# Macaron block on one core: q and k rows by frequency and then head, one store for each unit, half of the first heads loaded later

## The chip, the cores and the metric

One core of one Trainium2 chip runs the whole program. The metric is the device time of one execution in microseconds (us).

## The reference

Input x is [2, 2048, 256]. LN is a layer norm without weights.

```
x = x + 0.5 * ffn(LN(x))          # 16 experts, each takes its 256 best tokens, and a shared expert
x = x + attn(LN(x))
x = x + 0.5 * ffn(LN(x))

attn: q, k, v = x @ W.T + b, 16 heads of 16; q, k rotated by position (cos, sin of 8 frequencies, halves of a head paired)
      att = softmax(causal(q k^T / 4));  y = att v;  return y @ Wo.T + bo
```

## The kernel before

The change lies in attention, which has three blocks of code: `projections`, `exact_shift` and `attention`. Each block ends with a barrier of all engines.

`projections` walks over 8 quads of 512 tokens (`q`). VectorE takes the statistics of a quad two ahead (`statistics`, L1350), ScalarE normalizes it (`normalize`), TensorE transposes it, ScalarE copies the columns (`columns`) and VectorE subtracts the copy for the low part (`low_columns`, L1371), since every product is made of three matmuls with high and low parts (`product3`, L182 to L184). TensorE then makes four tiles of rows, `rows(4q)` to `rows(4q + 3)`: the first halves of q's heads, the second halves, and the same for k. VectorE rotates them (`rotate`, L1383) into `turns`. A unit `n = 2q + a` (a = 0 for q, 1 for k) is two such tiles: GpSimd forms the two sums (`turned`, L1448 and L1449), ScalarE makes the high half (`high`, L1308), GpSimd the low half (`low`, L1453), for the last three units VectorE instead (L1415), and SP stores the unit (`store`, L1190) into `q_rows` or `k_rows` in memory, in four transfers of 256 KB. Four units are in flight in `half`. The rows in memory lie head by head: 32 rows for a head, 16 high and 16 low, each 2048 tokens (8 KB) long.

SP works through one queue. For each q it first issues `load(q + 3)`, the x of the quad three ahead, which waits for the normalizing of quad q; then `store(2q)` and `store(2q + 1)`, which each wait for the low half. After each store of q = 4 and 5 it loads one of the four heads of attention's group 0 (`load_head`, L1590, and `load_shift`, L1602): 32 and 16 rows into 48 partitions, for q and for k. The rows of batch 0 are all stored by then.

At the end VectorE takes the largest squared norm of all heads (`largest`, L1423 to L1429) and leaves a flag `unsafe`. `exact_shift` is a guarded stage: SP, GpSimd, VectorE and TensorE read the flag and jump over the stage if it is 0, which it is for these inputs. Its loop over all 32 heads would compute exact maxima.

`attention` has 8 groups of 4 heads and for each 4 blocks of 512 queries. A unit is a set of scores (L1826, L1834) that ScalarE turns into exponentials (L1905); the scores of a unit wait for the exponentials of the unit three before. Block 0 of group 0 has 5 units, block 1 has 13, so block 2 begins at unit 18. Block 0 and 1 read columns 0 to 1023 of queries and keys only. SP waits for GpSimd to clear the buffer of group 1 and loads group 1, then the output weights, the biases and four residuals; group g is loaded when group g - 2 has had its scores.

## Time and profile before

| | |
|---|---|
| median of 3 runs | 1627.05 us |
| lowest and highest | 1625.15 and 1629.43 us |
| the profiled execution, its time | 1620.89 us |
| its span in the trace | 1619.2 us |
| mean granted clock of TensorE | 0.983 |
| busy: TensorE, ScalarE, VectorE, GpSimd | 93%, 61%, 55%, 35% |

Busy time is the time covered by instructions of an engine. [...] Engines in rows: PE is TensorE's matmul, PEld its weight load, DVE VectorE, ACT ScalarE, POOL GpSimd, SPq the queue on which SP issues transfers.

### The profile page before, as it was taken

What the parts mean: (1) busy time and instruction counts of PE and PEld (TensorE: products, weight loads), DVE (VectorE), ACT (ScalarE), POOL (GpSimd) and SP (SyncE); (2) the same over time, 40 slices, a digit from 0 to 9 for tenths busy, and PEclk for the clock granted to TensorE, in tenths of its full rate; (3) what the DMA queues carried; (4) which work ended last, traced back from release to release, by engine and by line L of the source; (5) the groups of instructions that cost most, each with busy time, mean ns of one, the idle gap of its engine ahead of it and who ended that gap; (6) DMA issues with size and microseconds to landing.
All of it is one profiled execution on the core that took longest, in us unless ns stands there. A gap on an engine that the chain in (4) does not pass through costs nothing. (4 is left out here: it accounts for less than half of the span.)

```text
span 1619.2 us, 26554 instructions
## 1 busy us (share of the span) xinstructions
PE 1508.0 (93%) x9945; PEld 1048.4 (65%) x9945; DVE 888.3 (55%) x1946; ACT 981.1 (61%) x1330; POOL 559.4 (35%) x498
## 2 busy tenths in 40 slices
PE   4899999999995878999999999999799999999997
PEld 3788889889884663333333333333588888898886
DVE  6787666667655771133043421212788757676663
ACT  7322254454434768999999999999532225544542
POOL 3000245665635872111011111110300035656644
PEclk9999999999997997999999999999999999999999
DMA  8231166666634799225054352210422136666753
GB/s 282 65 99 53 51 166 148 156 146 154 152 65 130 219 239 229 41 42 81 7 103 85 121 84 38 43 53 27 145 71 96 49 103 154 149 151 151 154 130 39
DMA packets 121552, 181.04 MB, mean 112 GB/s; under 512 B 19600, under 2 KB 83600, under 8 KB 118288
## 3 DMA queue, kind: packets, MB, share of 16 engines
q1 hardware_dynamic: 92960, 130.57, 31.0%
q0 software_dynamic: 28464, 48.78, 14.8%
q8 instruction: 79, 1.29, 0.4%
q14 instruction: 49, 0.40, 0.1%
HBM read 123.73 MB, written 55.57 MB: 111 GB/s over the span
## 5 line engine op out<-in xcount | busy, mean ns | idle before, releaser
L1905 ACT ACTIVATE 8072_pr<-8072_pS 128x1024 f32<-128x1024 f32 x448 | 421.2, 1073 | 12.9 <-PE 8072_pS L1826 11.6
L1856 PE MATMUL 8072_pO<-8072_pr,6212_vres 128*32 128x512 f32 x1792 | 240.3, 606 | 4.9 <-DVE 8072_tO L1930 3.8
L1826 PEld LDWEIGHTS 8072_pS<-sq_rows,sk_rows 50*128 50x128 f32 x896 | 74.5, 185 | 198.0 <-ACT 8072_pr L1905 153.4
L1826 PE MATMUL 8072_pS<-sq_rows,sk_rows 50*128 50x512 f32 x896 | 185.1, 465 | 8.3 <-ACT 8072_prs L1905 4.1
L1930 DVE STREAM_TRANSPOSE 8072_tO<-8072_pO 128x512 f32<-128x512 f32 (+1 forms) x33 | 23.0, 698 | 265.2 <-PE 8072_pO L1856 265.2
L182 PE MATMUL 112_pGU<-columns_XT,weights_wts 128*128 128x512 f32 x384 | 153.0, 398 | 1.6 <-DVE columns_XT L917 1.6
L182 PE MATMUL 15018_pGU<-columns_XT,weights_wts 128*128 128x512 f32 x384 | 152.5, 397 | 1.6 <-DVE columns_XT L917 1.6
L1919 POOL TENSOR_SCALAR_AFFINE_SELECT 8072_pr<-8072_pr 128x512 f32<-128x512 f32 x32 | 21.4, 670 | 376.0 <-ACT 8072_pr L1905 375.9
L183 PE MATMUL 112_pGU<-columns_XT,weights_wts 128*128 128x512 f32 x384 | 150.1, 391 | 0.0
L184 PE MATMUL 112_pGU<-columns_XT,weights_wts 128*128 128x512 f32 x384 | 150.0, 391 | 0.0
L183 PE MATMUL 15018_pGU<-columns_XT,weights_wts 128*128 128x512 f32 x384 | 149.8, 390 | 0.0
L184 PE MATMUL 15018_pGU<-columns_XT,weights_wts 128*128 128x512 f32 x384 | 149.8, 390 | 0.0
L764 ACT ACTIVATE hidden_hT<-15018_hf 128x512 fp32r<-128x512 f32 x96 | 60.7, 632 | 145.0 <-DVE 15018_hf L907 145.0
L764 ACT ACTIVATE hidden_hT<-112_hf 128x512 fp32r<-128x512 f32 x96 | 60.7, 632 | 144.7 <-DVE 112_hf L907 144.7
L1079 POOL DMA_INDIRECT out<-15018_eo,15018_idx x64 | 109.4, 1709 | 98.6 <-issue 67.1
L1079 POOL DMA_INDIRECT x_after_ffn<-112_eo,112_idx x64 | 109.4, 1709 | 98.2 <-issue 66.7
L182 PE MATMUL 112_pD<-weights_wts,hidden_hT 128*128 128x256 f32 x376 | 108.7, 289 | 1.4 <-DVE hidden_hT L912 1.4
L182 PE MATMUL 15018_pD<-weights_wts,hidden_hT 128*128 128x256 f32 x376 | 108.7, 289 | 1.4 <-DVE hidden_hT L912 1.4
L907 DVE TENSOR_TENSOR 15018_hf<-15018_gl,15018_pGU 128x512 f32<-128x512 f32 x96 | 65.9, 686 | 75.6 <-PE 15018_pGU L184 46.4
L907 DVE TENSOR_TENSOR 112_hf<-112_gl,112_pGU 128x512 f32<-128x512 f32 x96 | 65.9, 686 | 75.2 <-PE 112_pGU L184 45.7
L184 PE MATMUL 112_pD<-weights_wts,hidden_hT 128*128 128x256 f32 x376 | 106.3, 283 | 0.0
L184 PE MATMUL 15018_pD<-weights_wts,hidden_hT 128*128 128x256 f32 x376 | 106.3, 283 | 0.0
(370 smaller groups left out, 3419.9 us busy)
## 6 DMA issues: line engine op xcount, KB each, us to landing
112_raw_g<-WgT SPq DMA_DIRECT2D x16, 512.0 KB, 4.1
112_raw_u<-WuT SPq DMA_DIRECT2D x16, 512.0 KB, 3.6
112_raw_d<-WdT SPq DMA_DIRECT2D x16, 512.0 KB, 3.9
q_rows<-rows_half SPq DMA_DIRECT2D x32, 256.0 KB, 3.5
k_rows<-rows_half SPq DMA_DIRECT2D x32, 256.0 KB, 5.1
sq_rows<-q_rows SPq DMA_DIRECT2D x32, 256.0 KB
sk_rows<-k_rows SPq DMA_DIRECT2D x32, 256.0 KB
15018_raw_g<-WgT SPq DMA_DIRECT2D x16, 512.0 KB, 3.9
```

What stands on the lines that cost most here:

```text
L182: pe.matmul(out, w_hi, x_hi, start=start, stop=False)
L183: pe.matmul(out, w_hi, x_lo, start=False, stop=False)
L184: return pe.matmul(out, w_lo, x_hi, start=False, stop=stop)
L764: s_hh.done(a.activation(hT[0][:, i % 2, f, :], hf[:, f % 2, :], ACT.Copy))
L907: s_mul.done(v.tensor_tensor(hf[:, f % 2, :], gl[:, f % 2, :], pU(f % 2), ALU.mult))
L1079: s_sc[k].part(g.indirect_dma_start(out, bass.IndirectOffsetOnAxis(rows_[:, q:q + 1], 0), eo[:, k, q, :], None, compute_op=ALU.add), 16)
L1826: m = t_.matmul(to[:, e, :], key, query, start=True, stop=True)
L1856: m = t_.matmul(pO[e * 32:(e + 1) * 32, off:off + wd], vres[:, (g // GB) * TPB + kt, at:at + 32], from_(e), start=n == first[j], stop=n == ...
L1905: s_exp.done(a.activation(to, pS[:, u % RING, :, :], ACT.Exp, scale=HD ** -0.5))
L1919: s_mask.done(g.affine_select(out=blk_, in_=blk_, compare_op=ALU.is_ge, fill=0.0, base=0, pattern=[[0, GH], [1, P]], channel_multiplier=-1))
L1930: s_copy.done(v.transpose(tO[:, part], pO[:, part]))
```

## The change

- Rows come by frequency and then head. On the host, weights, biases and rope table are permuted (`by_half`, `c_rope`), and the mask that sums squares by head (`head_of`) is formed with a stride. In memory row r of head h now lies at r * 16 + h, so the rows of one head are 128 KB apart.
- A unit is stored in one transfer of 1 MB instead of four of 256 KB; `half` is one tensor, `both`.
- Quad 0 of x is loaded in two transfers instead of four; the rope table's last three parts share a semaphore, on which the second quad waits for all three.
- Of group 0's heads the projections load columns 0 to 1023 only. Attention issues the other columns as 16 transfers ahead of group 1, and the scores of group 0's block 2 wait for all of them (`s_rest`).
- The two sums of the last unit move from GpSimd to VectorE. VectorE's last work is in a new order: the sums, `low(13)`, the maxima, `low(14)`, the flag, `low(15)`.
- ScalarE ends the projections with a one-element exp.
- `exact_shift` writes its loop twice, once for each batch.

```diff
-        tab, ds = self.qk[a], self.bass.ds
+    def head_rows(self, a, b):
+        return self.qk[a].rearrange("(b n h) s -> b n h s", b=B, h=H)[b]
...
+        tab, ds = self.head_rows(a, b), self.bass.ds
         for lo, n in ((0, 2 * HD), (2 * HD, HD)) if a == 0 else ((0, HD), (HD, 2 * HD)):
-            eng.dma_start(dst[lo:lo + n, :].bitcast(self.f32), tab[ds(head * (2 * HD), n), :]).then_inc(sem, 16)
+            eng.dma_start(dst[lo:lo + n, :].bitcast(self.f32), tab[0:n, ds(head - b * H, 1), :]).then_inc(sem, 16)
...
-            half = [self.rows_at(f"half{h}", [P, KS, 2, W], f32r, 16 * 1024 * h) for h in range(2)]
+            both = self.rows_at("halves", [P, KS, 2, 2, W], f32r)
+            half = [both[:, :, h, :, :] for h in range(2)]
...
-                    for part in range(2):
-                        for u in range(2):
-                            dst = self.qk[a_].rearrange("(b h r u f) s -> b r u h f s", b=B, r=2, u=2, f=HD // 2)[bb][part][u]
-                            self.s_rows[n % KS].part(sp.dma_start(dst[:, :, cc * W:(cc + 1) * W],
-                                                                  half[part][:, n % KS, u, :].bitcast(f32)), 16)
-
-                for j in range(4):
-                    s_x0[j].done(sp.dma_start(xq[:, 0, j, :], xv[0][:, j, :]))
+                    dst = self.qk[a_].rearrange("(b n p) s -> b p n s", n=4, b=B)[bb]
+                    from_ = both[:, n % KS, :, :, :].rearrange("p h u w -> p (h u) w").bitcast(f32)
+                    self.s_rows[n % KS].done(sp.dma_start(dst[:, :, cc * W:(cc + 1) * W], from_))
+
+                for j in range(2):
+                    s_x0[j].done(sp.dma_start(xq[:, 0, 2 * j:2 * j + 2, :], xv[0][:, 2 * j:2 * j + 2, :]))
...
-                    s_trig[k].done(sp.dma_start(trig[:, :, part], self.ins["c_rope"][:, :, part]))
+                    s_trig[min(k, 1)].done(sp.dma_start(trig[:, :, part], self.ins["c_rope"][:, :, part]))
...
-                        if q in (4, 5):
+                        if (q, half_) in HEAD_AFTER:
+                            hh = HEAD_AFTER.index((q, half_))
                             sp.wait_ge(*s_clear.at(3))
                             sp.wait_ge(*s_zero.at(1))
-                            self.load_head(sp, 0, 2 * (q - 4) + half_)
-                            self.load_shift(sp, 0, 2 * (q - 4) + half_)
+                            self.load_head(sp, 0, hh, slice(0, S // 2), self.s_ld[0][hh // 2])
+                            self.load_shift(sp, 0, hh)
...
-                    a.wait_ge(*s_y.at(n + 1))
+                    a.wait_ge(*(s_y.at(n + 1) if n < 2 * J - 1 else s_last_y.at(1)))
...
                 high(2 * J - 1)
+                a.activation(warm[:, :], self.eps[0:1, :], ACT.Exp)
...
-                for n in range(POOL_LOW, 2 * J):
-                    self.s_rows[n % KS].wait(v, n // KS)
-                    low(n)
+                k = (2 * J - 1) % 3
+                s_turn.wait(v, 4 * J)
+                v.tensor_tensor(turns[k][:, 0, :], turns[k][:, 0, :], turns[k][:, 2, :], ALU.subtract)
+                s_last_y.done(v.tensor_tensor(turns[k][:, 1, :], turns[k][:, 1, :], turns[k][:, 3, :], ALU.add))
+                low(POOL_LOW)
                 largest(J - 1)
                 s_norm.wait(v, J // 2)
                 s_top.done(v.tensor_reduce(top[:, :], norm[:, :], AX.X, ALU.max))
+                low(POOL_LOW + 1)
...
                 s_flag.done(v.tensor_scalar(self.unsafe[:, :], prod[:, :], SAFE_NORMS, None, ALU.is_gt))
+                low(POOL_LOW + 2)
                 v.wait_ge(*s_flag.at(3))
...
-                for n in range(2 * J):
+                for n in range(2 * J - 1):
                     turned(n)
...
-                with eng.Fori(0, B * H) as h:
-                    body(h)
+                for b in range(B):
+                    with eng.Fori(b * H, (b + 1) * H) as h:
+                        body(b, h)
...
+                for hh in range(GH):
+                    self.load_head(sp, 0, hh, slice(S // 2, S), self.s_rest)
                 sp.wait_ge(*self.s_clear.at(4))
...
+                    if (g, blocks[j][1]) == (0, QB // 2) and "rest" not in arrived:
+                        arrived.add("rest")
+                        t_.wait_ge(*self.s_rest.at(1))
...
-    by_half = lambda w: w.reshape(H, 2, HF, -1).transpose(1, 0, 2, 3).reshape(D, -1)
+    by_half = lambda w: w.reshape(H, 2, HF, -1).transpose(1, 2, 0, 3).reshape(D, -1)
...
-        "c_rope": np.ascontiguousarray(np.tile(rope.transpose(2, 0, 1), (H, 1, 1))),
+        "c_rope": np.ascontiguousarray(np.repeat(rope.transpose(2, 0, 1), H, 0)),
```

## Rows read from the trace of the kernel before

**Rows 1.** The page's busy times: busy us (share of the span), instructions.

```profile
PE 1508.0 (93%) x9945; PEld 1048.4 (65%) x9945; DVE 888.3 (55%) x1946; ACT 981.1 (61%) x1330; POOL 559.4 (35%) x498
```

**Rows 2.** Timeline of VectorE in the loop: start, duration, instruction, [idle before, releaser].

```profile
537.93 1.41 DVE L1350 BATCH_NORM_STATS2 6217_st<-6217_xq 128x6 f32<-128x256 f32 x4 [1.34 <-DMA 6217_xq<-x_after_ffn]
...
540.74 1.29 DVE L1371 TENSOR_TENSOR sk_xT<-6217_pX,sk_xT 128x512 fp32r<-128x512 f32 x2 [0.85 <-ACT sk_xT L1297]
...
552.20 1.29 DVE L1371 TENSOR_TENSOR sk_xT<-6217_pX,sk_xT 128x512 fp32r<-128x512 f32 x2 [0.85 <-ACT sk_xT L1297]
...
562.16 1.41 DVE L1350 BATCH_NORM_STATS2 6217_st<-6217_xq 128x6 f32<-128x256 f32 x4 [1.21 <-DMA 6217_xq<-x_after_ffn]
...
564.97 1.29 DVE L1371 TENSOR_TENSOR sk_xT<-6217_pX,sk_xT 128x512 fp32r<-128x512 f32 x2 [0.85 <-ACT sk_xT L1297]
```

**Rows 3.** The loads of x, L1178: who waited for them, us, times.

```profile
  DVE 6217_st L1350: 2.8, 3
```

**Rows 4.** Timeline of VectorE, ScalarE, GpSimd and SP at the end of the projections.

```profile
600.82 1.21 DVE L1415 TENSOR_TENSOR rows_half<-sq_turns,rows_half 128x1024 fp32r<-128x1024 f32 x1
...
602.12 1.20 ACT L1316 ACTIVATE 6212_vres<-6217_pV 128x256 f32<-128x256 f32 x4
...
603.12 2.24 POOL L1449 TENSOR_TENSOR sq_turns<-sq_turns 128x512 f32<-128x512 f32 x1
...
606.55 1.22 DVE L1415 TENSOR_TENSOR rows_half<-sq_turns,rows_half 128x1024 fp32r<-128x1024 f32 x1 [2.31 <-ACT rows_half L1308]
607.69 0.68 DVE L1389 TENSOR_REDUCE 6217_norm<-6217_pN 128x1 f32<-128x512 f32 x1
607.80 2.48 SPq L1190 DMA_DIRECT2D k_rows<-rows_half  x4
...
609.53 0.14 DVE L1429 TENSOR_SCALAR 6212_unsafe<-6217_prod 1x1 int32<-1x1 f32 x1
```

**Rows 5.** Timeline at the start of attention, and where group 0 ends.

```profile
612.80 1.28 ACT L1905 ACT_TABLE_LOAD   x1 [6.35 <-PEq L1473]
...
612.84 1.22 PE L1826 MATMUL 8072_pS<-sq_rows,sk_rows 50*128 50x512 f32 x4 [3.84 <-PEq L1473]
...
614.10 1.94 ACT L1905 ACTIVATE 8072_pr<-8072_pS 128x1024 f32<-128x1024 f32 x2
...
631.70 0.73 PE L1826 MATMUL 8072_pS<-sq_rows,sk_rows 50*128 50x512 f32 x4
...
678.09 0.80 SPq L1590 DMA_DIRECT2D sq_rows<-q_rows  x2
```

**Rows 6.** Timeline of SP's queue: start and duration of the issues, how many.

```profile
500.05 0.59 SPq L1178 DMA_DIRECT2D 6217_xq<-x_after_ffn  x1
500.67 2.90 SPq L1200 DMA_DIRECT2D 6217_trig<-c_rope  x3
...
530.55 2.48 SPq L1190 DMA_DIRECT2D k_rows<-rows_half  x4
533.08 0.59 SPq L1178 DMA_DIRECT2D 6217_xq<-x_after_ffn  x1
```

**Rows 7.** Stretches: us, busy of each engine, granted clock, DMA share, GB/s.

```profile
531.75:532.00 0.25, 0.00 (x0) 0.00 (x0) 0.25 (x1) 0.25 (x1) 0.00 (x0) 1.00 0.98 221
534.25:534.50 0.25, 0.25 (x2) 0.19 (x1) 0.00 (x0) 0.25 (x2) 0.25 (x1) 1.00 0.55 180
...
600.90:612.80 11.90, 1.93 (x14) 0.93 (x12) 5.89 (x8) 3.48 (x7) 4.38 (x3) 0.73 1.04 332
612.80:627.05 14.25, 12.95 (x80) 5.64 (x80) 1.40 (x3) 12.68 (x13) 7.39 (x8) 0.63 0.95 205
618.00:638.00 20.00, 19.42 (x156) 6.79 (x156) 2.79 (x6) 17.94 (x20) 4.90 (x8) 0.86 1.02 151
```

**Rows 8.** Timeline at the barrier behind attention, where no guarded stage follows.

```profile
1141.94 1.55 SPq L1762 DMA_DIRECT2D x_after_attn<-rows_acc  x2
1143.90 1.28 ACT L719 ACT_TABLE_LOAD   x1 [10.32 <-PEq L1620]
```

More of the change, by code:

```diff
@@ L171, in scope, with load_stack @@
         return st
-    def load_stack(self, eng, dst, a, head, sem):
-        tab, ds = self.qk[a], self.bass.ds
+    def head_rows(self, a, b):
+        return self.qk[a].rearrange("(b n h) s -> b n h s", b=B, h=H)[b]
+    def load_stack(self, eng, dst, a, b, head, sem):
+        tab, ds = self.head_rows(a, b), self.bass.ds
         for lo, n in ((0, 2 * HD), (2 * HD, HD)) if a == 0 else ((0, HD), (HD, 2 * HD)):
-            eng.dma_start(dst[lo:lo + n, :].bitcast(self.f32), tab[ds(head * (2 * HD), n), :]).then_inc(sem, 16)
+            eng.dma_start(dst[lo:lo + n, :].bitcast(self.f32), tab[0:n, ds(head - b * H, 1), :]).then_inc(sem, 16)
     def product3(self, pe, out, w_hi, w_lo, x_hi, x_lo, start, stop):
@@ L1161, in projections @@
             s_n0 = sig("proj_act_first")
-            s_x0 = [sig(f"proj_x_first{j}", 16) for j in range(4)]
-            s_trig = [sig(f"proj_trig{k}", 16) for k in range(S // W)]
+            s_x0 = [sig(f"proj_x_first{j}", 16) for j in range(2)]
+            s_trig = [sig("proj_trig_first", 16), sig("proj_trig", 16)]
             s_T, s_Q, s_V, s_N, s_tt = (sig("proj_pe_" + n_) for n_ in ("T", "Q", "V", "N", "top"))
@@ L1168, in projections @@
             s_wh, s_wl, s_y, s_lo = (sig("proj_pool_" + n_) for n_ in ("wh", "wl", "y", "lo"))
-            s_last = sig("proj_dve_lo")
+            s_last, s_last_y = sig("proj_dve_lo"), sig("proj_dve_y")
             POOL_LOW = 2 * J - 3
+            HEAD_AFTER = ((4, 0), (4, 1), (5, 0), (5, 1))
             s_clear = self.s_clear
@@ L1378, in rotate @@
                     if n < 4 * (S // W):
-                        v.wait_ge(*s_trig[q].at(1))
+                        v.wait_ge(*(s_trig[1].at(S // W - 1) if q else s_trig[0].at(1)))
                     s_lo.wait(v, n // 2 - 2)
@@ L1393, in _ @@
                 with nc.allow_low_precision(reason="zeros and ones"):
-                    s_set.done(v.tensor_reduce(head_of[:, 0:H], self.ident[:, :].rearrange("p (h w) -> p h w", w=HD // 2), AX.X, ALU.add))
+                    s_set.done(v.tensor_reduce(head_of[:, 0:H], self.ident[:, :].rearrange("p (w h) -> p h w", h=H), AX.X, ALU.add))
                 statistics(0)
@@ L1505, in run, with head @@
                         self.s_ld[0][pair].wait(sp, 1)
-                    def head(h):
+                    def head(b, h):
                         sp.wait_ge(s_go, h + 1)
-                        self.load_stack(sp, qa, 0, h, s_ld)
-                        self.load_stack(sp, ka, 1, h, s_ld)
+                        self.load_stack(sp, qa, 0, b, h, s_ld)
+                        self.load_stack(sp, ka, 1, b, h, s_ld)
                         dve_h.wait(sp, "lo", h)
@@ L1535, in run, with head @@
                     v.sem_inc(s_go, 1)
-                    def head(h):
+                    def head(b, h):
                         v.wait_ge(s_ld, 64 * h + 64)
@@ L1563, in run, with head @@
                     t_.wait_ge(s_ident, 1)
-                    def head(h):
+                    def head(b, h):
                         with t_.Fori(0, TPB) as q:
@@ L1577, in _, with load_head @@
                 guarded(t_, run)
-    def load_head(self, sp, g, hh):
+    def load_head(self, sp, g, hh, cols, loaded):
         k, pair, base = g % 2, hh // 2, 64 * (hh % 2)
@@ L1586, in load_head @@
                 self.s_rows[n].wait(sp, self.stored(2 * NQ // B if g < 4 else 2 * NQ, n))
-        head, loaded = g * 4 + hh, self.s_ld[k][pair]
+        head = g * 4 + hh
         for a_, dst in enumerate((self.sq, self.sk)):
             for lo, n in ((0, 2 * HD), (2 * HD, HD)) if a_ == 0 else ((0, HD), (HD, 2 * HD)):
-                loaded.part(sp.dma_start(dst[base + lo:base + lo + n, k, pair, :].bitcast(self.f32),
-                                         self.qk[a_][head * 2 * HD:head * 2 * HD + n, :]), 16)
+                loaded.part(sp.dma_start(dst[base + lo:base + lo + n, k, pair, cols].bitcast(self.f32),
+                                         self.head_rows(a_, head // H)[0:n, head % H, cols]), 16)
     def stored(self, units, n):
@@ L2054, in attn @@
             self.unsafe = st.sb("unsafe", [1, 1], self.i32)
-            self.s_rows = [sig(f"rows_stored{k}", 64) for k in range(ROWS_RING)]
+            self.s_rows = [sig(f"rows_stored{k}", 16) for k in range(ROWS_RING)]
+            self.s_rest = sig("rest", 16 * 16)
             self.s_ld = [[sig(f"loaded{k}{pair}", 16 * 10) for pair in range(2)] for k in range(2)]
```

8 lines of the change are left out of this document (4 added, 4 removed).

## The prediction

> **What bounds the kernel now.** I read the page first [rows 1]: TensorE has records for 93% of the span, ScalarE for 61%. The edit touches the projections (496.56 to 610.28 us) and the first microseconds of attention, so the rest of the span can only be shifted. Then I read the stretches, the timeline of each engine and the waits in that part.
>
> Three things stand there. In the projections the quads follow each other through the two `low_columns` subtractions of VectorE: they start at 540.74 and 552.20, a period of 11.46 us, and at 564.97, a period of 12.77 us [rows 2]. The long period holds a wait of 1.21 us for the next 512 rows of x, an earlier one, at 537.93, a wait of 1.34 us [rows 2]; three such waits sum to 2.8 us [rows 3]. In the loop no other wait is for a transfer. At the end of the stage there is a chain: the GpSimd sum of the last unit (603.12, 2.24 us beside busy VectorE), ScalarE's high half right behind it at 605.4, VectorE's low half at 606.55, then four store issues of SP from 607.80 to 610.28. VectorE itself has its flag at 609.67. All engines start attention at 612.80, 2.52 us behind SP [rows 4, 5]. There the first exp stands behind a table load, although its scores were begun at 612.84 [rows 5].
>
> **The change, step by step.**
>
> *The store in one transfer.* SP issued four transfers a unit, 2.48 us together, and behind those of an odd unit the load of x [rows 6]. The new transfer has 512 pieces of 2 KB. Nearest rows: a load of 512 pieces of 1 KB took 0.59 us to issue, three of 256 pieces of 2 KB took 2.90 us, 0.97 each [rows 6]. I take 0.8 us; the bounds are 0.59 us and 2.48 us, if the issue goes by pieces as 4 x 0.62 does. So SP is free 1.7 us sooner for each unit.
>
> *The load of x that stands behind it.* It is issued 1.7 us sooner, but it need not land 1.7 us sooner, since its data come behind the data of the store. In the period read, the store was issued at 530.55, its data moved from 531.75 to about 534.2, the load was issued at 533.08, the share of the DMA engines dipped to 0.55 at 534.25 between the two, and VectorE went on at 537.93 [rows 2, 6, 7]. The megabyte of the store takes 2.5 us or more whoever issues it. So what is gained is the dip and the slow start behind it: 0.4 us at least. If the load then runs at the store's 2.5 us a megabyte, its data have moved at 535.5 and the whole wait (1.34, 1.21) goes. I take 0.9 us for each of the two waits and 0.2 for the third: **-2.0 us**, with bounds 0 (the issue isn't shorter, or the one big store holds the load back) and -3.1. The upper bound is the sum of waits, 2.8, and what the long periods are longer by beyond their wait, 0.1 each. That these microseconds reach the end: the period without a wait is 11.46 as it stands, and it needs nothing that the longer one doesn't.
>
> *First loads of x in two, the three later parts of the rope table on one semaphore.* Two issues take the place of four. The statistics read half a megabyte in the same order, and each half now lands in one. The gain of the last half and the loss of the first are each about one issue, 0.59 us at most [rows 6]. I take 0. The later rope parts are issued by 503.6, and the second quad turns more than ten microseconds later: 0. The head mask's reduction reads with a stride now; VectorE has idle time there till the first x lands: 0.
>
> *Row order.* Weights, biases, rope table and mask are permuted on the host, so no instruction of compute changes. What changes is that a head's 48 rows lie 128 KB apart instead of 8 KB. The loads of heads run at 151 GB/s with the share of the DMA engines at 1.02 [rows 7]; stores reach far more. I take the rate as unchanged. [...]
>
> *Last sums on VectorE.* Two 512-column sums cost half of the 1.21 us of a 1024-column subtraction [rows 4], 0.65 each with a start. From 600.82: sums to 602.2, low half of unit 13 to 603.4, maximum (0.68) and a short reduction to 604.3, low half of unit 14 to 605.5 (TensorE turns the tops under it), best, product and flag, three short ones of which the last took 0.14, to 606.2, low half of unit 15 to 607.4 [rows 4]. That last one needs ScalarE's high half, which stands behind the values' eviction (602.12, 1.20 us) and so ends at 604.4: covered. GpSimd drops out, so neither its 2.24 us nor a stretched subtraction occurs. SP issues at 607.4 and is done at 608.2 with 0.8 us; before it was 610.28. **-2.1 us**; bounds -2.3 (issue of 0.59) and -0.4 (2.48). Neither part does it alone: with the sums alone SP would end at 607.4 + 2.48 = 609.9, with the one transfer alone VectorE would be last, at 609.67.
>
> *Exp ahead of the barrier.* ScalarE is idle from 604.4 on, the load of 1.28 us and a one-element exp fit under the rest. At attention's start the first exp began at 614.10, 0.02 us behind the table load. Its scores are half of four matmuls that took 1.22 us from 612.84, so 613.5 [rows 5]. **-0.5 us**; bounds 0 (TensorE, at a low clock, then sets the pace) and -0.6. [...]
>
> *Second halves of the columns moved behind the barrier.* 16 transfers (4 heads x 2 x 2) with 1.57 MB leave the projections and go ahead of group 1 in attention. In the projections nothing waited for them, so nothing is gained there but a shorter backlog of stores (share 1.04 from 600.90 to 612.80 [rows 7]). In attention the queues passed are: SP's own for group 1 (20 issues, held back by GpSimd's clear), then the output weights and four residuals. Two issues of this kind take 0.80 us [rows 5], so the 16 take 6.4; the data of group 1, 3.15 MB and 21 us at 151 GB/s, come behind. It is first needed when group 0 has had its scores, at 678.09 [rows 5]; by this rate all has landed by 644. Covered by over 30 us. The second halves are needed by unit 18, at 631.70 less 2.6, so 629.1 (the loop's gain shifts both sides alike). The second halves are issued from 610.7, move behind the last store from about 611.9, and 1.57 MB at 151 GB/s are 10.4 us: landed at 622.6. Covered by 6 us: 0.
>
> *Guarded stage with its loops written twice.* It is skipped, but its code is jumped over. The barrier with it takes 2.52 us; the one behind attention, without a guarded stage, 0.41 (from 1141.94 + 1.55 to 1143.90) [rows 8]. The 2.1 us between is what the test and the jump cost. A few dozen more instructions lie under it: 0, bounds -0.3 and +0.5.
>
> *Clock.* [...] ScalarE is idle for 1.57 of the 14.25 us of the stretch in attention [rows 7], which is all that the low clock can cost it there; I take 0, bounds -0.8 and +0.8.
>
> **Sum.** -2.0 - 2.1 - 0.5 = -4.6 us. The profiled execution took 1620.89 us with a span of 1619.2, so it would be 1616.3. It lies 6.16 us under the median of the runs shown, 1627.05; the median would be 1622.4, faster by 0.28%. About 0.3%, 4.9 us, is what a measurement of this kernel can tell from no change, and the forecast stands at that edge.
>
> **The rivals.**
>
> *All of it comes* (0.25). The waits for x go wholly (-3.1), the issue takes 0.59 us (-2.3), the table gives 0.6 and the clock 0.8: -6.8, 1620.2. For it: the dip and the slow start behind the store. Against: the load's data still stand behind a megabyte.
>
> *One big transfer is no cheaper to issue* (0.11). 512 pieces cost 2.48 us. Then the waits stay, SP ends at 609.9: -0.4 - 0.5, 1626.1. For it: 128 pieces cost 0.62 here. Against: 512 pieces of 1 KB cost 0.59.
>
> *The second halves come late* (0.08). The rate of the head loads falls with the pitch. Down to 91 GB/s they still land by 629.1 and nothing shows. At 60 GB/s they land at 638.1, a stall of 9.0 us, and group 1, 3.15 MB, lands 52.5 us later at 690.6 where it is needed at 678.09 - 2.6 + 9.0 = 684.5: 6.1 more. -4.6 + 15.1 = +10.5, 1637.5. It decides for slower at about 64 GB/s. Against: the limit in the trace looks like one of few partitions written (full share at 151 GB/s where stores of all partitions moved 332 in [rows 7]), which the pitch leaves alone. [...]
>
> *The load of x waits longer* (0.06). One entry of a megabyte keeps the load's pieces back, so that the load lands 1 us later than now in each of five periods: +5.0 - 2.6 = +2.4, 1629.5. For it: the load's first data are slow even now, a share of 0.55 behind a store [rows 7]. Against: fewer and earlier issues can't by themselves make data later.
>
> **How the numbers follow.** The forecast has 0.50, with its own range 1620.5 to 1624.5 (the x term from -0.8 to -2.6, the barrier and the clock). It falls on either side of 4.9 us in the shares 0.22 and 0.28. Faster: 0.22 + 0.25 = 0.47. Slower: 0.07 of the late halves and 0.01 of the longer wait, 0.08. The same: 0.45. The range of 8 in 10 goes from 1619.0 to 1627.5: it takes in most of "all of it", the forecast and the dear issue, and leaves out the late halves and the far end of the gains.
>
> **What would show it.** Right: one SP row of 0.6 to 1.0 us for each unit; waits for x under 0.5 us each; GpSimd without a row behind 600; SP's last issue within 1 us of VectorE's last low half; no table load at L1905; the unit 18 scores without a wait for a transfer. Wrong: store rows of 2 us or more; a wait of VectorE for x of a microsecond or more; TensorE idle about 19 us into attention; a barrier much over 2.5 us; a new drop of the clock inside the loop.

## The result, and the profile after

| | before | after |
|---|---|---|
| median, same chip | 1627.59 us (4 executions) | 1617.16 us (4 executions) |
| lowest and highest | 1625.15 and 1629.43 us | 1615.93 and 1619.29 us |
| ratio, 95% interval | | 0.9944 [0.9928, 0.9959] |
| the profiled execution, its span | 1620.89, 1619.2 us | 1619.29, 1617.5 us |

The change makes the kernel faster by 0.56%. By the ratio that is 9.1 us; 4.6 us had been forecast, and the median lies under the range of 1619.0 to 1627.5. The two profiled executions alone, 1620.89 and 1619.29 us, would have said 1.6 us. The first of them is none of the four in the table and lies 4.3 us under their lowest; the second is the slowest of its four. So the question is not only what the change gives, but what one execution can tell.

The page of after, busy us of each engine, share of the span, instructions:

```profile
PE 1513.9 (94%) x9945; PEld 1051.7 (65%) x9945; DVE 888.1 (55%) x1948; ACT 981.3 (61%) x1331; POOL 555.2 (34%) x496
```

The work is that of [rows 1]. What differs is where engines wait. The timeline of VectorE in the loop, after (start, duration, instruction, idle before and its releaser):

```profile
538.28 1.41 DVE L1356 BATCH_NORM_STATS2 6217_st<-6217_xq 128x6 f32<-128x256 f32 x4 [0.55 <-DMA 6217_xq<-x_after_ffn]
541.09 1.29 DVE L1377 TENSOR_TENSOR sk_xT<-6217_pX,sk_xT 128x512 fp32r<-128x512 f32 x2 [0.85 <-ACT sk_xT L1302]
552.55 1.29 DVE L1377 TENSOR_TENSOR sk_xT<-6217_pX,sk_xT 128x512 fp32r<-128x512 f32 x2 [0.85 <-ACT sk_xT L1302]
561.70 1.41 DVE L1356 BATCH_NORM_STATS2 6217_st<-6217_xq 128x6 f32<-128x256 f32 x4 [0.40 <-DMA 6217_xq<-x_after_ffn]
```

VectorE's waits for x are 0.55 and 0.40 us, and the third one is gone; they were 1.34 and 1.21, 2.8 in all [rows 2, 3]. Now SP's queue after, the same stretch (start and duration of the issues, how many):

```profile
531.70 0.38 SPq L1195 DMA_DIRECT2D k_rows<-rows_halves  x1
532.12 0.51 SPq L1184 DMA_DIRECT2D 6217_xq<-x_after_ffn  x1
```

One megabyte is issued in 0.38 us, where the four quarters took 2.48 [rows 6]. The end of the projections and the start of attention after, timelines of VectorE, ScalarE and SP:

```profile
599.87 0.69 DVE L1426 TENSOR_TENSOR sq_turns<-sq_turns 128x512 f32<-128x512 f32 x1
...
603.21 1.28 ACT L1345 ACT_TABLE_LOAD   x1
...
604.62 0.14 DVE L1438 TENSOR_SCALAR 6212_unsafe<-6217_prod 1x1 int32<-1x1 f32 x1
604.70 1.20 DVE L1421 TENSOR_TENSOR rows_halves<-sq_turns,rows_halves 128x1024 fp32r<-128x1024 f32 x1
605.92 0.37 SPq L1195 DMA_DIRECT2D k_rows<-rows_halves  x1
...
609.78 1.94 ACT L1921 ACTIVATE 8175_pr<-8175_pS 128x1024 f32<-128x1024 f32 x2 [5.07 <-PE 8175_pS L1842]
```

SP is through 3.99 us earlier (606.29, before 610.28), the table load stands under VectorE's tail, and the first exp waits for its scores and for nothing else: 609.78 in place of 614.10 [rows 5], 4.32 us earlier. To this point the total is near the sum's 4.6, but its terms are not as forecast. From the start of the projections to VectorE's first instruction behind the last rotation (600.82 before, 599.87 after) only 0.96 us are gained, and from there to the first exp 3.37. In the loop the waits for x are 1.85 us shorter, but the second `low_columns` began at 517.60 in place of 516.46, since TensorE's granted clock rose later. The same three microseconds, first before, then after (us, busy of each engine, granted clock, DMA share, GB/s):

```profile
511.00:514.00 3.00, 3.00 (x19) 2.56 (x18) 2.98 (x6) 0.91 (x2) 0.17 (x1) 1.00 0.61 221
```

```profile
511.00:514.00 3.00, 3.00 (x10) 2.34 (x10) 1.85 (x3) 0.69 (x1) 0.00 (x0) 0.50 0.42 149
```

In the five profiled executions of each kernel that are compared below the second `low_columns` begins 19.8 to 21.0 us into the stage before and 20.0 to 21.0 after, so this is chance, and that the total agreed to 0.3 us is partly luck. The stretches at the stage's end, after (us, busy of each engine, granted clock, DMA share, GB/s):

```profile
596.00:606.00 10.00, 5.67 (x38) 4.42 (x36) 9.29 (x15) 7.49 (x12) 3.49 (x3) 1.00 0.63 216
606.00:612.80 6.80, 3.35 (x18) 2.37 (x18) 0.00 (x0) 3.02 (x4) 3.85 (x2) 0.51 1.02 352
```

The DMA engines have room (0.63) where they were full before: of the kernel before the same view gives

```profile
596.00:606.00 10.00, 6.45 (x42) 5.17 (x40) 7.48 (x8) 5.67 (x10) 8.93 (x5) 1.00 1.01 241
```

The forecast read a full share here, in [rows 7], and took it for harmless.

### The profile page after: what moved, and what is told of

It is laid out like the page before. It is cut to its first block and busy times, and to the rows that moved or that the text cites. A ratio compares the mean times of both kernels' runs of the same rounds, so it can differ in the third digit from the quotient of the medians.

```text
span 1617.5 us, 26521 instructions
## 1 busy us (share of the span) xinstructions
PE 1513.9 (94%) x9945; PEld 1051.7 (65%) x9945; DVE 888.1 (55%) x1948; ACT 981.3 (61%) x1331; POOL 555.2 (34%) x496
## 5 line engine op out<-in xcount | busy, mean ns | idle before, releaser
L1921 ACT ACTIVATE 8175_pr<-8175_pS 128x1024 f32<-128x1024 f32 x448 | 421.9, 1075 | 20.7 <-PE 8175_pS L1842 19.5
L1872 PE MATMUL 8175_pO<-8175_pr,6212_vres 128*32 128x512 f32 x1792 | 240.8, 608 | 4.7 <-DVE 8175_tO L1946 3.9
L1842 PEld LDWEIGHTS 8175_pS<-sq_rows,sk_rows 50*128 50x128 f32 x896 | 74.9, 186 | 201.6 <-ACT 8175_pr L1921 153.6
L1842 PE MATMUL 8175_pS<-sq_rows,sk_rows 50*128 50x512 f32 x896 | 186.3, 468 | 10.3 <-PEq L1483 5.5
L1946 DVE STREAM_TRANSPOSE 8175_tO<-8175_pO 128x512 f32<-128x512 f32 (+1 forms) x33 | 23.0, 698 | 267.8 <-PE 8175_pO L1872 267.8
L186 PE MATMUL 15142_pGU<-columns_XT,weights_wts 128*128 128x512 f32 x384 | 152.5, 397 | 1.6 <-DVE columns_XT L921 1.6
L187 PE MATMUL 15142_pGU<-columns_XT,weights_wts 128*128 128x512 f32 x384 | 149.9, 390 | 0.0
L188 PE MATMUL 15142_pGU<-columns_XT,weights_wts 128*128 128x512 f32 x384 | 149.8, 390 | 0.0
L768 ACT ACTIVATE hidden_hT<-15142_hf 128x512 fp32r<-128x512 f32 x96 | 60.7, 632 | 144.4 <-DVE 15142_hf L911 142.9
L1083 POOL DMA_INDIRECT out<-15142_eo,15142_idx x64 | 109.6, 1712 | 98.6 <-issue 67.1
L186 PE MATMUL 15142_pD<-weights_wts,hidden_hT 128*128 128x256 f32 x376 | 108.8, 289 | 1.4 <-DVE hidden_hT L916 1.4
L911 DVE TENSOR_TENSOR 15142_hf<-15142_gl,15142_pGU 128x512 f32<-128x512 f32 x96 | 65.9, 687 | 75.0 <-PE 15142_pGU L188 49.3
L188 PE MATMUL 15142_pD<-weights_wts,hidden_hT 128*128 128x256 f32 x376 | 106.3, 283 | 0.0
```

Source lines behind the costliest of these rows:

```text
L186: pe.matmul(out, w_hi, x_hi, start=start, stop=False)
L187: pe.matmul(out, w_hi, x_lo, start=False, stop=False)
L188: return pe.matmul(out, w_lo, x_hi, start=False, stop=stop)
L768: s_hh.done(a.activation(hT[0][:, i % 2, f, :], hf[:, f % 2, :], ACT.Copy))
L911: s_mul.done(v.tensor_tensor(hf[:, f % 2, :], gl[:, f % 2, :], pU(f % 2), ALU.mult))
L1083: s_sc[k].part(g.indirect_dma_start(out, bass.IndirectOffsetOnAxis(rows_[:, q:q + 1], 0), eo[:, k, q, :], None, compute_op=ALU.add), 16)
```

## Experiments

Kernels in one table ran on the same chip beside the same executions of the kernel before.

### Parts undone

**The change as it is.**

> The changed kernel once more, beside the kernel before on the same chip. Theory A (the gain is what the two traces show up to the start of attention's group 2, 4.0 us, and the rest of the first result is that single executions differ by drops of TensorE's clock elsewhere): 4 to 5.5 us faster, ratio 0.9966 to 0.9975, and executions of either kernel with the same mean granted clock differ by 4 to 5 us. Rival B (the change also takes something out of attention or the second feed-forward part that the profiled executions hide): 8 to 11 us faster again, 0.993 to 0.995, at equal granted clocks too.

**Four store transfers again**, in the new row order, otherwise the changed kernel:

```diff
-                    self.s_rows[n % KS].done(sp.dma_start(dst[:, :, cc * W:(cc + 1) * W], from_))
+                    for k in range(4):
+                        self.s_rows[n % KS].part(sp.dma_start(dst[:, k, cc * W:(cc + 1) * W], from_[:, k, :]), 16)
```

> The changed kernel with the unit stored in four transfers again. Theory A: SP issues 1.5 us or so for a unit instead of 0.4, the waits for x come back to some 1.2 us each and the last store ends 2 us later, so 3 to 4 us slower than the changed kernel. Rival B (the halved columns carry the gain, as they empty the queue of transfers): less than 1 us slower than the changed kernel.

**Whole rows of the first heads** again, nothing left for attention:

```diff
-                            self.load_head(sp, 0, hh, slice(0, S // 2), self.s_ld[0][hh // 2])
+                            self.load_head(sp, 0, hh, slice(0, S), self.s_ld[0][hh // 2])
...
-                for hh in range(GH):
-                    self.load_head(sp, 0, hh, slice(S // 2, S), self.s_rest)
```

> The changed kernel with whole rows of the first group loaded in the projections and none behind the barrier. Theory A (the halves are covered on both sides): the same time as the changed kernel within 1 us. Rival B (the halves carry part of the gain, through the issue of the stores and the barrier, which stand in a full queue): 2 to 5 us slower than the changed kernel, with the gap from SP's last issue to attention longer than in the changed kernel.

**Last sums on GpSimd**, and VectorE's end in the old order:

```diff
-                v.tensor_tensor(turns[k][:, 0, :], turns[k][:, 0, :], turns[k][:, 2, :], ALU.subtract)
-                s_last_y.done(v.tensor_tensor(turns[k][:, 1, :], turns[k][:, 1, :], turns[k][:, 3, :], ALU.add))
...
-                for n in range(2 * J - 1):
+                for n in range(2 * J):
                     turned(n)
```

> The changed kernel with the last sums and the old order of the end (GpSimd's sums, low halves of units 13 to 15, maxima, flag). Theory A: VectorE's flag is last again, near 608.5 us in the trace where the changed kernel has its last low half at 605.9, so 2 to 3 us slower than the changed kernel. Rival B (the barrier waits for something else, the transfers): less than 1 us slower.

| before here 1623.36 us | median (lowest to highest), executions | ratio, 95% interval |
|---|---|---|
| the change | 1615.58 (1614.73 to 1617.94), 6 | 0.9947 [0.9928, 0.9966] |
| four stores | 1620.56 (1615.78 to 1625.14), 12 | 0.9979 [0.9965, 0.9993] |
| whole rows | 1621.88 (1615.60 to 1626.00), 12 | 0.9988 [0.9971, 1.0005] |
| sums on GpSimd | 1620.40 (1614.55 to 1624.82), 12 | 0.9979 [0.9964, 0.9993] |

Each undone part seems to cost 5 to 6 us of a gain of 8, which can't all be so. The lowest times lie within 1.3 us of each other. In the one profile of each kernel the time from the start of the projections to the first exp is 113.06 us with the change, 117.14 with four stores, 114.28 with whole rows and 114.87 with the sums on GpSimd: there the parts cost 4.1, 1.2 and 1.8 us. Either the parts work only together, or the six executions of the full change were luckier than most. That asked for it once more.

### The change again, and single parts

> The changed kernel once more, in full, to see whether its ten times so far (1614.7 to 1619.3 us) lie together by chance. Theory 'spread is chance': every kernel of this family has the same scatter of about 9 us above its lowest time, from drops of the TensorE clock behind waits in attention that stand in all of them. Then this run has times up to 1623, a median of 1618 to 1619, and a ratio near 0.9970 (1623.4 less the 4.6 us that the timelines show is 1618.8). Theory 'the full change is less exposed': the times stay under 1619.5, the median is again 1615.5 to 1616.5, the ratio 0.995. The lowest time is about 1614.7 by both.

**The row order only** (with four stores, whole rows, the old tail, no early exp, and x's first quad in two transfers):

> Of the change only the new order of the rows in DRAM (by frequency and then head) and what follows from it for the loads of the heads, with two first loads of x in place of four; four store transfers a unit, whole rows of the first heads, last sums on GpSimd and no exp ahead are as before. Theory of the prediction: 0, so a median within 1 us of the kernel before (ratio 0.9994 to 1.0006) and a lowest time within 0.7 us of its lowest. Rival 'the order is what helps': loads of the heads with rows far apart are quicker or disturb attention less, 2 us or more below before (ratio under 0.9988). Rival 'the order costs': each group's loads wait longer, 1 us or more above.

**The row order and the single store only:**

> The new row order and the unit stored in one transfer; whole rows of the first heads, the last sums on GpSimd, no exp ahead. By the timelines: the waits for x shrink by about 1.9 us and the last store ends in 0.4 us in place of 2.5, but VectorE's flag, which stood 0.6 us ahead of the end of the stores, then ends the stage, so the end of the projections gains 0.6 us on top. Sum -2.5 us: lowest time about 1616.8, median about 1620.9, ratio 0.9985. Rival 'the store is all': ratio 0.9970 or less. Rival 'only together': ratio over 0.9995.

**No exp ahead of the barrier:**

```diff
-                a.activation(warm[:, :], self.eps[0:1, :], ACT.Exp)
```

> The changed kernel without the exp of one element at the end of the projections, so the table load of 1.28 us stands again before the first exp of attention. Theory: the first exp starts later by the table load less the wait for the first scores, 0.4 to 0.5 us, so 0.4 us over the full change at the lowest (1615.1) and at the median of the same call. Rival 'the whole table load is on the path': 1.3 us above. Rival 'spread': the median lies 3 us or more above the full change though the first exp moves by under 1 us, as for the parts undone so far.

| before here 1626.04 us | median (lowest to highest), 12 executions each | ratio, 95% interval |
|---|---|---|
| the change again | 1619.92 (1614.75 to 1625.69) | 0.9952 [0.9934, 0.9971] |
| row order only | 1619.64 (1615.46 to 1622.04) | 0.9956 [0.9940, 0.9972] |
| row order and single store | 1619.88 (1617.11 to 1624.18) | 0.9966 [0.9949, 0.9983] |
| no early exp | 1618.95 (1616.09 to 1626.32) | 0.9958 [0.9940, 0.9976] |

The spread is the same for the full change, so the narrow six were chance and "only together" falls. The medians of the first table can't rank the parts. Nor can the two tables be set against each other to 0.2%: row order and single store are contained in "whole rows" of the first table and yet have the better ratio, 0.9966 against 0.9988 (0.9985 had been expected from the timelines). By its median the kernel without the early exp can't be told from the full change; what the exp gives, 0.42 us, only the profile shows. The surprise is the second line: the order of the rows, put down at 0, by itself does about what the whole does. SP's queue in the order-only kernel shows how (same view as above):

```profile
530.99 1.80 SPq L1196 DMA_DIRECT2D k_rows<-rows_halves  x4
532.83 0.56 SPq L1184 DMA_DIRECT2D 6217_xq<-x_after_ffn  x1
```

The same four transfers of 256 KB take 1.80 us to issue, not 2.48. The waits for x in that kernel, from its list of waits between 515 and 590 us (who waited for what: us in all, times, longest):

```profile
DVE 6217_st L1356 <- DMA 6217_xq<-x_after_ffn: 0.5, 2, 0.3
```

2.8 us have become 0.5. In the profile of the kernel with four stores of the first table they are 0.9 in all, not the 1.2 each that had been expected, and with the single transfer 0.7 to 1.0. So in the new order four transfers leave no more waiting for x than one does. Whether the single transfer would shorten the waits in the old order was not tried.

To the first exp this profile takes 114.90 us, where the five executions of the kernel before that are shown below take 120.2 in the mean. 4.4 us of the 5.3 are in the loop (100.99); the tail behind it, 13.91 us, lies within the range of before (13.28 to 19.02), and there one group of four issues took 4.64 us.

### The load of x alone

Each load of x in the loop stands behind two stores in SP's queue, although its buffer is free before them. One edit puts it in front:

```diff
+                load(3)
                 for q in range(J):
-                    if q + 3 < J:
-                        load(q + 3)
+                    if q + 4 < J:
+                        load(q + 4)
```

> The changed kernel with each later load of x issued in front of the two stores that it stood behind, one quad sooner (its buffer has been read by then). What is left of VectorE's waits for x in the loop, 0.55 and 0.40 us, goes: lowest time about 1613.8, 0.9 us under the full change of the same kind (ratio 0.9945 where the full change has 0.9952 to 0.995). Rival 'waits for x bring clock drops with them': 2 us or more under the full change. Rival 'the load now delays the store': same or slower.

> The kernel before with that one edit only: each later load of x in front of the two stores (four transfers each, old row order). The three waits for x, 2.8 us together, should go from the loop, and nothing else moves. Theory 'a wait costs what it lasts': -2.8 us, ratio 0.9983, lowest time about 1617. Rival 'a wait also brings down the clock behind it': -4 to -6 us, ratio 0.9963 to 0.9975, and a higher mean clock. Rival 'the row order gained elsewhere than in these waits': as the first here, and the profile still has the store's 2.48 us and the stage's end as before.

Beside them ran the kernel before as a kernel of its own:

> The kernel before, unchanged, as a kernel of its own, for a second profiled execution and for the comparison with itself. Theory 'the one profiled execution was a lucky one': the ratio is 1.000 within 0.0015 and the median 3 to 6 us above the 1620.9 us of the execution that the forecast was summed on; the new profile shows the same waits for x in the projections (three, 2.5 to 3 us) and more stretches at the granted clock of 0.5. Rival 'something other than the clock differs from execution to execution': equal stretches at 0.5, and a longer wait somewhere else.

| before here 1627.3 us | median (lowest to highest), executions | ratio, 95% interval |
|---|---|---|
| x sooner, in the changed kernel | 1619.03 (1611.85 to 1623.50), 10 | 0.9947 [0.9927, 0.9967] |
| x sooner, in the kernel before | 1623.83 (1618.09 to 1626.79), 12 | 0.9974 [0.9955, 0.9992] |
| the kernel before again | 1627.06 (1621.13 to 1633.92), 12 | 0.9998 [0.9979, 1.0018] |

In the kernel before the edit gives 3.5 us by the medians and 4.2 by the ratio. Its interval, 1.3 to 7.3 us, has room for the 2.8 us that the waits lasted and for the dearer rivals. The profile of this kernel has no wait for x, and its loop takes 100.99 us, 2.8 less than the shortest of the five executions of before shown below. The granted clock in the loop (same view as above) is

```profile
520.00:598.00 78.00, 69.30 (x411) 55.71 (x411) 59.40 (x126) 58.38 (x111) 64.88 (x41) 1.00 0.72 197
```

In the changed kernel no wait for x is left, and the lowest time of all kernels, 1611.85 us, is its. Its ratio can't be told from the changed kernel's: it beats the kernel before; whether it beats the changed one is open. In its profile the first exp comes 110.54 us after the start of the projections, 2.8 less than the changed kernel's mean.

### More executions of each kernel under the profiler

> A third profiled execution of the kernel before. By 'lucky execution': between 1622 and 1628 us, the projections and attention with the same waits as the first one, and 3 to 10 us more at the granted clock of 0.5 than the 50 or so of the first from the projections on. By the rival: no such difference.

> A fourth profiled execution of the kernel before. In two of three so far the TensorE clock fell in the loop of the projections right behind waits for x, and the stage took 119.3 and 119.7 us to the first exp, against 117.5 in the execution that the forecast was summed on. Theory 'the waits for x bring the clock down in most executions': again 119 to 120 us with two stretches at 0.5 between 540 and 580 us; attention 519.5 us. Rival 'it is spread over all stages': 117.5 us here and the difference elsewhere.

> A fifth profiled execution of the kernel before: as the fourth, 119 to 120 us by the one theory, 117.5 by the other.

> A fourth profiled execution of the changed kernel (so far 113.1, 113.1, 114.0 us from the start of the projections to the first exp; attention 519.0 to 523.1 us, by where a clock drop falls). Theory: 113 to 114 us, at most one stretch at 0.5 in the loop, attention 519 to 523. Rival 'spread over all stages': more than 115 us in some executions, too.

> A fifth profiled execution of the changed kernel: as the fourth, 113 to 114 us, attention 519 to 523 us. With these the stage means of five executions each can be set against the difference of the medians, about 8 us: by the first theory the projections carry 5 to 6 of them.

Their times were 1624.22, 1625.14 and 1622.33 us (before) and 1616.21 and 1614.52 us (changed). With the first profiles there are five executions of each. I cut them at four points of the timelines: VectorE's clearing of the head mask (L1391, after L1397) at the start of the projections; its first instruction behind the last rotation; the first exp; the end of the last exp.

| | before, five executions | mean | changed, five executions | mean |
|---|---|---|---|---|
| until the projections | 496.6, 497.4, 497.5, 495.1, 495.9 | 496.5 | 496.6, 499.0, 499.6, 497.0, 496.5 | 497.7 |
| projections to the last rotation | 104.19, 105.87, 105.80, 103.82, 107.22 | 105.38 | 103.23, 103.17, 104.15, 103.46, 103.14 | 103.43 |
| from there to the first exp | 13.28, 13.82, 13.49, 19.02, 14.68 | 14.86 | 9.91, 9.89, 9.86, 9.91, 9.93 | 9.90 |
| attention | 519.5, 519.4, 519.6, 520.1, 518.0 | 519.3 | 523.1, 519.0, 521.3, 519.1, 518.3 | 520.1 |
| the rest | 485.6, 485.9, 486.2, 485.4, 484.8 | 485.6 | 484.7, 485.2, 485.7, 485.0, 485.0 | 485.1 |

The first number in each list is the execution of the first profile, so the forecast was summed on a tail of 13.28 us, the shortest of five. The changed kernel's tail is the same in all five to 0.07 us. What a longer tail of before is made of, in the one of 19.02 us (wait list from 590 to 616 us, then ScalarE's and SP's timelines):

```profile
ACT rows_half L1308 <- DMA k_rows<-rows_half: 5.9, 1, 5.9
```

```profile
607.35 1.06 ACT L1308 ACTIVATE rows_half<-sq_turns 128x1024 fp32r<-128x1024 f32 x1 [5.94 <-DMA k_rows<-rows_half]
```

```profile
600.15 5.28 SPq L1190 DMA_DIRECT2D k_rows<-rows_half  x4
605.48 4.80 SPq L1190 DMA_DIRECT2D q_rows<-rows_half  x4
610.33 3.78 SPq L1190 DMA_DIRECT2D k_rows<-rows_half  x4
```

The four issues that took 2.48 us take up to 5.28, and ScalarE can't write its high half, since the unit that had this place in the ring of four has not left. In the execution with the tail of 14.68 us the last two issues took 3.17 and 3.80 us. The stretch in the execution with the tail of 19.02 us:

```profile
596.00:606.00 10.00, 4.55 (x33) 3.63 (x31) 6.07 (x6) 4.87 (x9) 7.03 (x5) 0.97 1.06 214
```

The DMA engines are full at 214 GB/s; the last head loads were issued from 594.07 to 596.33 us, the next stores from 596.38. (In the execution of the first profile they were full as well, 1.01 at 241 GB/s, and no engine waited for a store.) The changed kernel with whole rows has the same picture, 1.02 at 209 GB/s and a wait of ScalarE of 3.7 us for a store, and its tail is 11.60 us, 1.7 us over the 9.9 of the full change. Of the nine profiles without the halves four have that wait, 3.4 to 5.9 us; of the eleven with the halves, in either order of rows, none.

The clock varies, too, but doesn't tell the kernel before from the changed one. Between the first quads and the last rotation it fell to 0.5 for 3.4 us once, twice, twice, once and twice in the five executions of before, and once, once and three times twice in those of the changed kernel. I had expected the drops to follow the long waits for x, after two executions of before. A single wait doesn't decide it: TensorE waited 2.08 us until 545.83 in the first execution of before and 2.07 us until 547.59 in the third; the third has a drop at 548.6 us, the first none. Over all twenty profiles, those of the next part included, waits and drops do go together. The four in which VectorE waits 0.5 us for x in the loop or not at all (row order only, x sooner in either kernel, halves and x sooner) have no drop there, with a granted clock of 1.00 in the mean from 520 to 598 us; the other sixteen, with 0.7 to 2.9 us of waiting, have one or two each (0.96 to 0.98). The loop takes 100.68 to 100.99 us in the four and 102.62 or more in the others. So the changed kernel's loop, 103.43 in the mean, still holds some 2.5 us, more than the 0.8 to 1.0 that VectorE waits for x. With one profile of each of the four kernels this is a strong hint that such a wait costs more than it lasts, and no proof.

### Two varying waits taken out of the kernel before

**Halves only**, old order of rows, four stores:

```diff
-                            self.load_head(sp, 0, 2 * (q - 4) + half_)
+                            self.load_head(sp, 0, 2 * (q - 4) + half_, slice(0, S // 2), self.s_ld[0][q - 4])
...
+                for hh in range(GH):
+                    self.load_head(sp, 0, hh, slice(S // 2, S), self.s_rest)
                 sp.wait_ge(*self.s_clear.at(4))
```

> The kernel before with the halves only: of the first four heads half the columns are loaded in the projections and the rest at the start of attention (old row order, four stores, x as it was; the three later parts of the rope table count on one semaphore). Five profiled executions of the kernel before took 117.5 to 122.8 us from the start of the projections to the first exp; in two of them the last stores of the stage were issued into a full queue (3.2 to 5.3 us for four issues that take 2.5 otherwise), and in one ScalarE waited 5.9 us for a store before. Theory 'the whole rows of the heads crowd the last stores': this goes, so 1.5 to 2 us under the kernel before (ratio 0.9988 to 0.999), no wait of ScalarE for a store, last stores at 2.5 us. Rival of the forecast, 'halves are worth nothing': ratio 0.9995 to 1.0005. Rival 'the old order's second halves come late in attention': slower.

**Halves, and x sooner:**

> The kernel before with two edits: halves as above, and each later load of x one quad sooner (alone it gave 0.9974). Theory 'the two waits that vary, for x and for the stores at the end, carry what the sum left out': 0.9974 times 0.999, that is 0.9960 to 0.9965, about 6 us, though neither the row order nor the one transfer nor the tail is changed; projections 115 to 116 us to the first exp. Rival 'the row order or the one transfer carries it': not under 0.9972.

| before here 1623.94 us | median (lowest to highest), executions | ratio, 95% interval |
|---|---|---|
| halves | 1622.36 (1618.20 to 1627.62), 12 | 0.9989 [0.9974, 1.0004] |
| halves and x sooner | 1617.33 (1615.41 to 1619.63), 6 | 0.9959 [0.9945, 0.9973] |

Alone the halves give 1.8 us, with an interval that holds nothing as well. Their profile has no wait of ScalarE for a store, but the last two issues still took 3.19 and 2.99 us and the tail 13.81, no less than in the first executions of before, so that half of the expectation missed. Together the two edits give 6.7 us where about 6 was expected (six executions only, as few as the narrow six above; to the first exp the profile takes 115.72 us). That is 0.41% against the 0.48 to 0.56% of the whole change, with the old order, four transfers and the old tail in place. With x sooner alone the loop had fallen to 100.99 us and the tail had grown to 16.12, with 4.0 us of ScalarE waiting for a store: it looks as if a faster loop runs into the full DMA engines (a share of 1.06 from 596 to 606 us), and the halves give part of that back (100.98 and 14.74). With one profile of each this is argued, not shown.

## Why the prediction was wrong

*The sum on its own execution.* At the first exp 4.6 was forecast and 4.32 measured. This is in part luck: the loop gave 0.96 for 2.0, as the clock rose later, and what follows it 3.37 for 2.6.

- The waits for x: -2.0. From three waits of 2.8 us, 0.95 is left, so 1.85. In the means of five the loop is 1.95 us shorter. Right in size, but the cause named isn't needed for it: I gave it to the single transfer, and the row order with four transfers leaves 0.5 us of waits by itself, 0.9 with the halves and the new tail beside it.
- The store's issue: 0.8 us taken, 0.37 measured, under my bound of 0.59. With four transfers in the changed kernel the tail was 13.08 us against 9.91: 3.2 us, of which the last group of issues, 2.69 for 0.37, is 2.3.
- The tail: -2.1. From the last rotation to the end of SP's last issue it was 9.46 us and is 6.42, so -3.0; the issue and VectorE's work, each about half a microsecond shorter than I took them, make the difference. VectorE's order came out as written (flag 604.76, last low half 604.70 to 605.90), and neither part does it alone: with the sums on GpSimd the flag ends the stage at 606.78 and the tail is 12.25 us.
- The early exp: -0.5; without it the tail is 10.33, so 0.42 us. In the profile without it the load began at 608.16 and took 1.28 us, the first exp followed at 609.45, and 0.42 of the 1.28 was on the path.
- The guarded stage: from SP's last issue (606.29) to TensorE's first matmul of attention (608.95) 2.66 us, where it was 2.56: +0.1.
- The second halves land in time: between 606 and 700 us TensorE has no wait for a transfer.

*The step that failed* is the one on the second halves of the columns: "In the projections nothing waited for them, so nothing is gained there but a shorter backlog of stores (share 1.04)". This put at nothing what the full DMA engines cost. In that execution nothing waited. In others the backlog is what sets the end: the share of 1.04 was the sign of a resource with no room. In one execution it cost nothing that could be seen, in another 5.7 us (19.02 less 13.28). The mean tail is 4.96 us shorter, where the first pair shows 3.37 and the sum had 2.6. How much of this the halves do is less sure: they alone gave 0.9989 with an interval that holds 1, but none of the eleven profiles with them has the wait for a store, which four of the nine without them have. With it fell *Row order*, "I take the rate as unchanged", which priced the loads of heads and left out the stores: in the loop four are issued in 1.80 us in place of 2.48, and the row order alone gives 0.9956.

*The step that carried the sum to the median* failed in the same way. The profiled execution lay 6.16 us under the median, and I shifted both alike. But part of what lifted the median of before were the long tails and loops that the change removes; the five executions of before have a mean of 1623.35 us, 2.5 above the one I used. Over five executions each the projections are 6.9 us shorter (1.95 + 4.96), against the 4.3 of the first pair.

*What stays open.* The spans of these executions differ by 5.3 us in the mean, the medians by 10.4, 7.8 and 6.1 us in three comparisons. Ahead of the projections the changed kernel took 1.2 us longer and in attention 0.8, with ranges of 2 to 5 us within the five executions, so chance can have made these. Up to 5 us of the difference of the medians is not placed by stages. Part of it goes with the clock. In two of the comparisons the changed executions had the higher granted clock in the mean, 0.9823 against 0.9799 and 0.9795 against 0.9780. A line through the times over the granted clocks, one slope for both kernels, gives as an estimate what is left at equal clocks: 6.1 and 5.2 us for the change (each to about 1.5), 3.2, 3.9 and 4.1 for the parts undone of the first table, 4.6 for the row order alone, and 0.5 for the kernel before beside itself. That is near the 6.9 of the stages, and undoing a part then costs 2 to 3 us, not 5 to 6. The clock can itself be an effect of the change, so the rest need not be chance. Nor can the parts be added: the row order alone and the halves with x sooner each give 0.4%, since both take the waits for x away; how much of the row order's share lies outside the loop is open. Why the order of rows makes four transfers cheaper to issue was not tried either.

*The rivals.* "All of it comes" was nearest (1620.2), and named the wrong reasons: two of the three waits for x stay, and the clock gave nothing (0.53 and 0.51 from 606.00 to 612.80). The dear big transfer is out, with 0.37 us. The late halves did not come: group 1 and the halves move at 159 GB/s between 620 and 640 us, at a share of 1.02, where the old order gives 144 at 1.01. That the rate falls with the pitch, which this rival supposed, no run shows: between rows 8 KB and 128 KB apart there is no loss. The longer wait for x did not come.

## What to carry to other kernels

In all five executions of the kernel before the DMA engines were full from 596 to 606 us (shares of 1.01 to 1.07), and the tail took 13.28 us in one and 19.02 in another. So price a queue or a set of DMA engines that a profile shows full also where no engine waits for it in that execution, by what happens when the next transfer finds it a microsecond fuller. Take two or three profiles of the kernel before, if they are to be had, and cut them at the same points; the stage whose length varies is where a change can gain more than one timeline shows. When an edit is put down at nothing, run it alone: the row order was one, and by itself gave 0.9956.

## What the runs showed of the hardware

*The same bytes, another order.* Four stores of 256 KB in pieces of 2 KB mostly took 2.48 us to issue in the old row order and 1.80 in the new, in the middle of the loop (at most 3.55 in the first profile of before, 3.05 in the profile with the new order only); all of it in one transfer took 0.37 to 0.42. At a DMA share near 1.0 four issues took up to 5.28 us in the old order and 4.64 in the new.

*A clock drop behind a wait in one execution, and none behind the same wait in another.* Once in attention, behind its first group, TensorE waits 1.55 us for VectorE. Here is that wait in the kernel with four stores (timeline of TensorE), then the four microseconds behind it (busy of each engine, granted clock, DMA share, GB/s):

```profile
691.04 0.36 PE L186 MATMUL 8223_pT<-8223_wo,turned_yT 128*128 128x256 f32 x1 [1.55 <-DVE turned_yT L1975]
```

```profile
692.00:696.00 4.00, 4.00 (x28) 1.26 (x32) 0.69 (x1) 2.97 (x4) 0.00 (x0) 0.60 0.98 158
```

The granted clock is 0.60 in the mean of this stretch, 0.90 in its first microsecond and 0.50 in the other three. In the kernel before the wait is as long, ends at 693.01, and the clock stays at 1.00 until 700. Where the drop came, the group took 68.6 us instead of 65.6. Such drops fall in other places in other executions: in the first profile of the changed kernel one stands behind a wait of 1.57 us that ends at 949.19 (a clock of 0.50 from 951 to 954 us), and its attention took 523.06 us where the others of five have 518.3 to 521.3. They are part of the spread of 7 to 13 us that the kernels here show over a dozen executions. What taking that wait away would give was not tried.
